# Graph layers of two batches interleaved ahead of the first attention, and the whole program written out by batch from a table

## The chip, the cores and the metric

One core of one Trainium2 chip runs the kernel. The metric is the device time of one execution in microseconds (us); three runs of the kernel before are at hand. The profile comes from one further look at one execution of it, with the hardware profiler on.

## The reference

For each of 4 batches, a two-layer graph attention runs over a context of 256 nodes, with the layer-normed `x` as its adjacency; its result is added to `x`. Then a layer norm and one transformer block follow (grouped-query attention with 16 heads on 4 key/value heads, then a top-2 mixture of 8 experts), again added to `x`.

```python
def gat_layer(x, adj, W, a_self, a_neigh, b):      # twice per batch; 8 heads of 32
    feat = jnp.einsum('nf,hfo->hno', x, W)
    e = (feat @ a_self)[:, :, None] + (feat @ a_neigh)[:, None, :]
    e = leaky_relu(e, 0.2) + -1e10 * (1.0 - adj)[None]
    out = jnp.einsum('hnm,hmo->hno', softmax(e), feat) + b[:, None, :]
    return elu(concat_heads(out))
x = x + gat(gat(ctx, layernorm(x)), layernorm(x))
h = rmsnorm(layernorm(x)); q, k, v = h @ qw.T, h @ kw.T, h @ vw.T
...
x = x + (hidden + moe_out)
```

## The kernel before

Two kinds of work are done for each batch. The **graph layers** (function `gat` of each engine) are laid out over 48 steps: layer 0 has its units at steps 5 to 12 and layer 1 at steps 28 to 35. A unit is two heads of one half of the nodes. TensorE (PE) makes the pairwise sums of a unit in the bank `zb` (L424), ScalarE (ACT) copies them to `zs` (L625), VectorE (DVE) applies the leaky relu to `lr` (L895) and adds the mask with a row minimum in `tt` (L904), GpSimd (POOL) subtracts that minimum (L735), PE turns the unit in `tb` (L432: four transposes), ACT takes the exponential into `gpT` (L630), and PE multiplies with the features in `ob` (L443: eight products of 33 columns). Ahead of the units of a layer stand the terms of the two attention vectors (L400), their three bf16 parts (L877 to L881, L408) and the features (L414); for layer 0 also the mask (L860 to L872). The layers end with the elu, the sum `x1`, and a preparation: a layer norm and an RMS norm whose inverse roots are iterated on POOL, and a transpose to `hT` (steps 44 to 47: L851, L937 to L950, L715 to L747, L455).

The **transformer block** (functions `fill`, `empty`, `part`) has steps of its own, from the QKV products (L509) at step 1 to the down products (L565) at step 47, in five PSUM banks.

The order on every engine is written by hand, as loops over the steps: first the graph layers of batch 0 alone (here called the **prologue**), then three turns of a hardware loop (**passes** 0, 1 and 2) whose step `s` holds step `s` of the graph layers of batch `b + 1` and step `s` of the block of batch `b`, then the block of batch 3 alone (the **last pass**). Each engine works strictly in its order and waits on semaphores. The loop is one body that all engines jump back to, with semaphore values worked out in registers:

```python
            for s in range(STEPS):
                ...
                gat(0, s)
            with pe.Fori(0, B - 1) as b:
                for s in range(STEPS):
                    gat(b + 1, s)
                    for w in work(s):
                        fill(b, w)
                    long_products(b, s)
            for s in range(STEPS):
                for w in work(s):
                    fill(B - 1, w)
                long_products(B - 1, s)
```

Of the kernel before, what the change touches and what calls it, by code (L numbers as in the profile page):

```python
# [7 lines left out]
BF16 = mybir.dt.bfloat16  # L8
ALU = mybir.AluOpType
# [26 lines left out]
C_CAUSAL = C_ID + P  # L36
C_COS = C_CAUSAL + P
C_SIN = C_COS + T * HD
C_PICK = C_SIN + T * HD
# [4 lines left out]
C_END = C_TRI + E * E  # L44
# [28 lines left out]
N_A, N_B, N_P = 39, 64, 36  # L73


STEPS = 48

# [71 lines left out]
BANKS = SLOW_BANKS + QUICK_BANKS  # L149
ORDER = [w for s in range(STEPS) for w in work(s)]  # L150
# [10 lines left out]
def block_program(nc, x, ctxT, w0, w1, gat_rows, norm_cols, qk_rows, wqkv, wo, wgate, wgu, wd, consts, spread, out):  # L161
    ctx = ExitStack()
    with ctx:
# [10 lines left out]
        cst = sb("cst", [P, C_END])  # L174
# [8 lines left out]
        qkw = sb("qkw", [P, 2 * HD])  # L183
# [8 lines left out]
        xin = sb("xin", [P, T, D])  # L192
        cin = sb("cin", [F_IN, N])
        stats = sb("stats", [P, T, 6])
        mv = sb("mv", [P, T, 2])
        rs_v = sb("rs_v", [P, 2 * T])
        rs_y = sb("rs_y", [P, 2 * T])
        rs_a = sb("rs_a", [P, 2 * T])
        maskv = sb("maskv", [P, T, N])
        feat = sb("feat", [P, T, H, FE])  # L200
        sn_res = sb("sn_res", [P, T, 2 * H])
        parts = sb("parts", [P, T, NP, 2 * H], BF16)
        partsT = sb("partsT", [KZ, N], BF16)
        pair_l = sb("pair_l", [KZ, N], BF16)
        pair_r = sb("pair_r", [KZ, H, N], BF16)
        zs = sb("zs", [P, 2, 2 * N])
        lr = sb("lr", [P, 2, 2 * N])
        tt = sb("tt", [P, 3, 2, N])
        gmn = sb("gmn", [P, 3, 2])
        gpT = sb("gpT", [P, 3, 2, T, P])  # L210
        gsum = sb("gsum", [P, H])
        go = rows[:, 2 * D:4 * D].rearrange("p (t d) -> p t d", t=T)
        gex = sb("gex", [P, T, D])
        wprod = gex[:, 0, :]
        x1 = sb("x1", [P, T, D])
        hid = sb("hid", [P, T, D])
        hn = gex
        hT = sb("hT", [P, KT, N])
        gT = hT
# [3 lines left out]
        v_sb = sb("v_sb", [P, T, HKV * HD])  # L223
        m1 = sb("m1", [P, 4, G * HD])
        m2 = sb("m2", [P, 4, G * HD])
        ssq = sb("ssq", [P, QU * G])
# [6 lines left out]
        qT = sb("qT", [P, HQ, N])  # L233
        kT = sb("kT", [P, HKV, N])
# [4 lines left out]
        prob = sb("prob", [P, 5, 2 * N])  # L239
        pT0 = sb("pT0", [P, G, P])  # L240
        pT1 = sb("pT1", [P, T, G, P])
# [14 lines left out]
        mixT = sb("mixT", [NP * E, N], BF16)  # L256
# [6 lines left out]
        zb = pb("zb", [P, 512])  # L263
        tb = pb("tb", [P, 512])
        ob = pb("ob", [P, 512])
        bank = [pb(f"bank{k}", [P, 512]) for k in range(BANKS)]


        in_cst, in_w0, in_gat, in_x, in_c = sem("in_cst"), sem("in_w0"), sem("in_gat"), sem("in_x"), sem("in_c")
        in_qkv, in_o, in_gu, in_d = sem("in_qkv"), sem("in_o"), sem("in_gu"), sem("in_d")  # L270
        out_free = sem("out_free")
        x_used, c_used = sem("x_used"), sem("c_used")

        setup_v, setup_done = sem("setup_v"), sem("setup_done")

        dve_a = sem("dve_a")
        z_full, z_free = sem("z_full"), sem("z_free")
        t_full, t_free = sem("t_full"), sem("t_free")
        parts_ready, pair_l_ready = sem("parts_ready"), sem("pair_l_ready")
        pair_r0_ready, pair_r1_ready = sem("pair_r0_ready"), sem("pair_r1_ready")  # L280
        lrelu_done, score_ready, shifted = sem("lrelu_done"), sem("score_ready"), sem("shifted")
        pv_done, o_free = sem("pv_done"), sem("o_free")
        gout_ready, gexp_ready, gres_ready, hn_ready = sem("gout_ready"), sem("gexp_ready"), sem("gres_ready"), sem("hn_ready")
        ln_seed, pool_a, ln_ready, hid_ready = sem("ln_seed"), sem("pool_a"), sem("ln_ready"), sem("hid_ready")
# [17 lines left out]
        def t_value(b, l, n):  # L302


            return b * 2 * (NU + 3) + l * (NU + 3) + n + 1

# [38 lines left out]
        def _(sp):  # L345
            sp.dma_start(w0x[:, 0:D], w0).then_inc(in_w0, 16)
            sp.dma_start(rows[:, 0:2 * D], gat_rows[:, 0:2 * D]).then_inc(in_w0, 16)
            sp.dma_start(cst[:, :], consts).then_inc(in_cst, 16)
            sp.dma_start(cin[:, :], ctxT[0]).then_inc(in_c, 16)
            sp.dma_start(xin[:, :, :], x[0].rearrange("(t p) d -> p t d", p=P)).then_inc(in_x, 16)  # L350
# [4 lines left out]
            sp.dma_start(qkw[:, :], qk_rows).then_inc(in_gat, 16)  # L355
# [7 lines left out]
            def load_inputs(b):  # L363
                sp.wait_ge(c_used, b)
                sp.dma_start(cin[:, :], ctxT[bass.ds(b, 1)].squeeze(0) if not isinstance(b, int) else ctxT[b]).then_inc(in_c, 16)
                sp.wait_ge(x_used, b)
                src = x[bass.ds(b, 1)].squeeze(0) if not isinstance(b, int) else x[b]
                sp.dma_start(xin[:, :, :], src.rearrange("(t p) d -> p t d", p=P)).then_inc(in_x, 16)

            def store(b):  # L370
                dst = out[bass.ds(b, 1)].squeeze(0) if not isinstance(b, int) else out[b]
                for t in range(T):
                    sp.wait_ge(y_ready, b * T + t + 1)
                    sp.dma_start(dst[t * P:(t + 1) * P, :], yo[:, t, :]).then_inc(out_free, 16)

            load_inputs(1)
            with sp.Fori(0, B - 2) as b:
                load_inputs(b + 2)
                store(b)
            store(B - 2)  # L380
            store(B - 1)
# [4 lines left out]
        def _(pe):  # L386
            def gat(b, a):

                for l in range(2):
                    operands = [(cin, w0x)] if l == 0 else [(gT[:, k, :], w1x[:, k, :]) for k in range(KT)]  # L390
                    if a == TERMS_AT[l]:
                        if l == 0:
                            pe.wait_ge(in_c, (b + 1) * 16)
                        else:
                            pe.wait_ge(t_free, t_value(b, 0, NU + 2) + 1)
                            pe.nop(nofuse=True)
                        pe.wait_ge(t_free, t_value(b, l, 0))
                        for t in range(T):
                            for i, (xt, w) in enumerate(operands):
                                mm = pe.matmul(tb[:, t * 2 * H:(t + 1) * 2 * H], xt[:, t * P:(t + 1) * P], w[:, D:D + 2 * H],  # L400
                                               start=(i == 0), stop=(i == len(operands) - 1))
                        mm.then_inc(t_full, 1)
                    if a == PARTS_AT[l]:
                        pe.wait_ge(parts_ready, b * 2 + l + 1)
                        pe.wait_ge(t_free, t_value(b, l, 1))
                        pe.nop(nofuse=True)
                        for t in range(T):
                            mm = pe.transpose(tb[0:KZ, t * P // 2:(t + 1) * P // 2].bitcast(BF16),  # L408
                                              parts[:, t, :, :].rearrange("p a c -> p (a c)"), identb[:, :])
                        mm.then_inc(t_full, 1)  # L410
                        pe.wait_ge(z_free, z_value(b, l, 0))
                        for t in range(T):
                            for i, (xt, w) in enumerate(operands):
                                mm = pe.matmul(zb[:, t * D:(t + 1) * D], xt[:, t * P:(t + 1) * P], w[:, 0:D],  # L414
                                               start=(i == 0), stop=(i == len(operands) - 1))
                        mm.then_inc(z_full, 1)
                    for k in units(l, a):
                        t, hp = divmod(k, H // 2)
                        if k == 0:
                            pe.wait_ge(pair_l_ready, b * 2 + l + 1)  # L420
                        if k < H // 2:
                            pe.wait_ge(pair_r0_ready if k < 2 else pair_r1_ready, b * 4 + l * 2 + k % 2 + 1)
                        pe.wait_ge(z_free, z_value(b, l, k + 1))
                        pe.matmul(zb[:, :], pair_l[:, t * P:(t + 1) * P],  # L424
                                  pair_r[:, 2 * hp:2 * hp + 2, :].rearrange("k h m -> k (h m)"), start=True, stop=True)\
                          .then_inc(z_full, 1)
                    for k in units(l, a - TRANS_LAG):
                        pe.wait_ge(shifted, unit(b, l, k) + 1)
                        pe.wait_ge(t_free, t_value(b, l, k + 2))
                        for h in range(2):  # L430
                            for m in range(T):
                                mm = pe.transpose(tb[:, (h * T + m) * P:(h * T + m + 1) * P],  # L432
                                                  tt[:, k % 3, h, m * P:(m + 1) * P], ident)
# [802 lines left out]
```

## Time and profile before

| | |
|---|---|
| runs | 679.01 us median of 3 (676.33, 679.01, 680.93) |
| profiled execution, span from first to last instruction | 676.1 us |
| mean granted TensorE clock | 0.944 |
| PE busy | 604.8 us (89%) |
| DVE busy | 441.0 us (65%) |
| POOL busy | 292.0 us (43%) |
| ACT busy | 266.7 us (39%) |

Of the profiled execution the span is the time that is known; it is 0.2 us under the fastest run and 2.9 us under the median. PE is the busiest engine, but the share is a mean over stages with different limits, so the stages are to be read one by one: the prologue up to the first QKV product at 100.21 us, the three passes, and the last pass from 559.00 us.

### The profile page before, as it was taken

Reading aid. Unit: us, or ns where it says so; the run is one execution under the profiler, and the core shown is the slowest. Engines: PE = TensorE matmul, PEld = TensorE weight load, DVE = VectorE, ACT = ScalarE, POOL = GpSimd, SP = SyncE. Lnnn points to the kernel's source line nnn. Section 1 sums busy time; section 2 is a strip of 40 time slices with the busy share of each in tenths; the row PEclk is TensorE's granted clock in tenths of the full one; section 3 lists DMA queues with packets and bytes.
Section 4 is the critical chain, followed back from the end, with each engine's and each line's share of the span. In section 5 each row is a group of like instructions: output and inputs, shape, how many; then the busy total and the mean of one; then the engine's idle time right before and its main releaser. Section 6 shows DMA issues by size and latency. Waiting matters only on the chain.

```text
span 676.1 us, 11574 instructions
## 1 busy us (share of the span) xinstructions
PE 604.8 (89%) x3140; PEld 445.9 (66%) x3140; DVE 441.0 (65%) x1277; ACT 266.7 (39%) x653; POOL 292.0 (43%) x588
## 2 busy tenths in 40 slices
PE   2786938979999998879999998879999998999998
PEld 1573933559678873558778973458777974676786
DVE  5727537975738756985738765986738766565363
ACT  2313305546533304636633304647633303674020
POOL 1514325885424023886425023886424126773000
PEclk9997558898999998979999998989999999999999
DMA  8900000000000000000000000000000000000000
GB/s 313 380 6 0 2 16 4 1 2 1 0 1 2 2 26 10 4 0 2 0 1 1 1 26 10 1 0 1 1 1 1 1 1 16 1 1 1 1 1 16
DMA packets 8305, 14.51 MB, mean 21 GB/s; under 512 B 860, under 2 KB 7068, under 8 KB 7988
## 3 DMA queue, kind: packets, MB, share of 16 engines
q1 hardware_dynamic: 8244, 13.76, 5.8%
q8 instruction: 31, 0.51, 0.3%
q14 instruction: 30, 0.25, 0.1%
HBM read 12.70 MB, written 1.05 MB: 20 GB/s over the span
## 4 chain that ended last, share of the span: by engine, by line
PE 56%; DVE 16%; issue 13%; POOL 9%; ACT 4%; POOLq 1%; DMA 1%; DVEq 0%; ACTq 0%; SPq 0%
PE bank L565 10%; PE bank L463 9%; PE ob L443 9%; PE bank L523 5%; PE tb L432 5%; PE bank L542 4%; DVE tt L904 3%; POOL m L775 2%; PE bank L538 2%; PE bank L534 2%; PE bank L509 2%; DVE lr L895 2%; PE zb L424 1%; ACT prob L666 1%; PE zb L414 1%
## 5 line engine op out<-in xcount | busy, mean ns | idle before, releaser
L735 POOL TENSOR_SCALAR tt<-tt,gmn 128x256 f32<-128x256 f32 x128 | 77.1, 613 | 64.1 <-DVE gmn L904 63.5
L509 PE MATMUL bank<-wqkv_sb,hT 128*128 128x512 f32 x192 | 97.9, 648 | 0.0
L666 ACT ACTIVATE prob<-bank,sneg,rms 128x128 f32<-128x128 f32 (+1 forms) x128 | 64.0, 507 | 68.5 <-DVE sneg L995 67.7
L775 POOL TENSOR_TENSOR m<-early,rope_s 128x256 f32<-128x256 f32 x80 | 70.8, 908 | 42.1 <-ACT early L647 41.8
L463 PE MATMUL bank<-m,wgu_sb 128*128 128x128 f32 (+1 forms) x480 | 86.6, 330 | 1.0 <-DVE m L1025 0.6
L791 POOL TENSOR_SCALAR prob<-prob,srcp 128x128 f32<-128x128 f32 (+1 forms) x128 | 53.7, 436 | 55.5 <-DVE srcp L1066 55.4
L463 PEld LDWEIGHTS bank<-m,wgu_sb 128*128 128x128 f32 x480 | 71.2, 191 | 9.2 <-issue 2.2
L443 PEld LDWEIGHTS ob<-feat,gpT 128*128 128x128 f32 x512 | 75.8, 227 | 0.8 <-issue 0.6
L443 PE MATMUL ob<-feat,gpT 128*128 128x33 f32 x512 | 75.2, 297 | 0.0
L895 DVE SCALAR_TENSOR_TENSOR lr<-zs 128x512 f32<-128x512 f32 x64 | 50.9, 797 | 25.3 <-ACT zs L625 22.6
L904 DVE CUSTOM_DVE_ANT_0 tt<-lr,maskv 128x256 f32<-128x256 f32 x128 | 62.3, 522 | 3.5 <-issue 2.9
L523 PE MATMUL bank<-kT,qT 128*128 128x128 f32 (+1 forms) x256 | 62.3, 360 | 0.9 <-ACT prob L666 0.9
L625 ACT ACTIVATE zs<-zb 128x512 f32<-128x512 f32 x64 | 38.3, 599 | 59.7 <-PE zb L424 56.5
L509 PEld LDWEIGHTS bank<-wqkv_sb,hT 128*128 128x128 f32 x192 | 36.3, 203 | 38.0 <-issue 35.0
L565 PE MATMUL bank<-wo_sb,qT 128*128 128x256 f32 x256 | 59.7, 383 | 0.3 <-ACT qT L672 0.3
L647 ACT ACTIVATE early<-bank 128x512 f32<-128x512 f32 x40 | 24.1, 603 | 89.8 <-PE bank L509 89.8
L565 PEld LDWEIGHTS bank<-wo_sb,qT 128*128 128x128 f32 x256 | 47.3, 190 | 10.0 <-issue 4.5
L432 PE MATMUL tb<-cst,tt 128*128 128x128 f32 x256 | 48.8, 322 | 4.6 <-ACT gpT L630 3.8
L523 PEld LDWEIGHTS bank<-kT,qT 128*128 128x128 f32 x256 | 41.4, 199 | 12.4 <-issue 6.3
L994 DVE TENSOR_REDUCE smx<-bank 128x2 f32<-128x512 f32 (+1 forms) x48 | 33.0, 686 | 24.8 <-PE bank L525 21.8
L630 ACT ACTIVATE gpT<-tb 128x512 f32<-128x512 f32 x64 | 38.4, 599 | 20.4 <-PE tb L432 19.9
L432 PEld LDWEIGHTS tb<-cst,tt 128*128 128x128 f32 x256 | 34.5, 169 | 17.1 <-issue 7.6
(151 smaller groups left out, 1026.5 us busy)
## 6 DMA issues: line engine op xcount, KB each, us to landing
wqkv_sb<-wqkv_dram SPq DMA_DIRECT2D x1, 3072.0 KB, 12.4
wgu_sb<-wgu_dram SPq DMA_DIRECT2D x2, 1408.0 KB, 11.2
wo_sb<-wo_dram SPq DMA_DIRECT2D x1, 2048.0 KB, 17.8
wd_sb<-wd_dram SPq DMA_DIRECT2D x1, 1408.0 KB, 15.6
xin<-x_dram SPq DMA_DIRECT2D x4, 256.0 KB, 2.7
out_dram<-rows SPq DMA_DIRECT2D x8, 128.0 KB, 1.9
rows<-gat_rows_dram SPq DMA_DIRECT2D x1, 512.0 KB
cst<-consts_dram SPq DMA_DIRECT2D x1, 425.0 KB, 3.6
```

The costliest lines, as they stand in the source:

```text
L432: mm = pe.transpose(tb[:, (h * T + m) * P:(h * T + m + 1) * P], tt[:, k % 3, h, m * P:(m + 1) * P], ident)
L443: mm = pe.matmul(ob[:, hh * FE:(hh + 1) * FE], gpT[:, k % 3, h, m, :], feat[:, m, hh, :], start=(m == 0), stop=(m == T - 1))
L463: mm = pe.matmul(ps[:, m * N + c0:m * N + c1], wgu_sb[:, m, k, n * P:(n + 1) * P], tokT[:, k, c0:c1], start=(k == 0), stop=(k == KT - 1))
L509: mm = pe.matmul(ps[:, :], hT[:, k, t * P:(t + 1) * P], wqkv_sb[:, k, c * G * HD:(c + 1) * G * HD], start=(k == 0), stop=(k == KT - 1))
L523: pe.matmul(ps[:, i * nk:(i + 1) * nk], qT[:, G * g + h, t * P:(t + 1) * P], kT[:, g, 0:nk], start=True, stop=False)
L565: mm = pe.matmul(bank_of(w)[:, 0:D], lhs[:, k, t * P:(t + 1) * P], rhs[:, k, :], start=(k == 0), stop=(k == end - 1))
L666: ins = act.activation(prob[:, n % 5, i * nk:(i + 1) * nk], ps[:, i * nk:(i + 1) * nk], ACT.Exp, bias=sneg[:, n, i:i + 1], scale=rq(g, t, ...
L735: ins = pool.tensor_scalar(tt[:, k % 3, h, :], tt[:, k % 3, h, :], -1.0, gmn[:, k % 3, h:h + 1], ALU.mult, ALU.add)
L775: ins = pool.tensor_tensor(dst[:, :, c, :], src[:, :, 1 - c, :], s_, ALU.mult)
L791: ins = pool.tensor_scalar(part_, part_, srcp[:, n, i:i + 1], 1.0, ALU.mult, ALU.mult)
L895: dve.scalar_tensor_tensor(lr[:, k % 2, :], zs[:, k % 2, :], 0.2, zs[:, k % 2, :], ALU.mult, ALU.min)\
L904: ins = dve.tensor_tensor_reduce(tt[:, k % 3, h, :], lr[:, k % 2, h * N:(h + 1) * N], maskv[:, t, :], 1.0, 3e38, ALU.add, ALU.min, gmn[:, ...
```

## The change

A table `PLAN` lists, step by step, whose work each engine issues, and every engine walks it without a loop. Ahead of the first block it holds the graph layers of batches 0 and 1, those of batch 1 two steps behind (`BEHIND`), and the preparation of batch 0. Pass 0 then carries the graph layers of batch 2, pass 1 those of batch 3, and passes 2 and 3 carry none; the preparation (`prep`) of the next batch stays at steps 44 to 47 of each pass.

For that, two sets of graph-layer buffers and semaphores exist. Set 0 (batches 0, 2 and 3) has buffers of its own; set 1 (batch 1 alone) is laid into tiles of the transformer block that are not in use yet (`qT`, `kT`, `v_sb`, `prob`, `pT0`, `pT1`) and into the PSUM banks 0 to 2. `x1` has three buffers, so that the sums of later batches can wait. `gT` and `hT` no longer share a tile. To make room, the rotary and causal tables are loaded into `x1` and `hid` at the start, and not kept in `cst`; this makes two more transfers in the setup, and the inputs of batch 1 are loaded there too.

```diff
+SET, SEQ, XS = (0, 1, 0, 0), (0, 0, 1, 2), 3
+BEHIND = 2
+PLAN = []
+for step in range(STEPS):
+    PLAN += [("gat", 0, step), ("gat", 1, step - BEHIND), ("prep", 0, step)]
...
+        PLAN += [("gat", batch + 2, step)] if batch + 2 < B else []
+        PLAN += [("prep", batch + 1, step)] if batch + 1 < B else []
+        PLAN += [("tail", batch, step)]
...
+        zb, tb, ob = [zb0, bank[0]], [tb0, bank[1]], [ob0, bank[2]]
...
+            sp.dma_start(angles, consts[:, C_COS:C_CAUSAL]).then_inc(in_gat, 16)
+            sp.dma_start(causal_in, consts[:, C_CAUSAL:C_END]).then_inc(in_gat, 16)
...
-            with pe.Fori(0, B - 1) as b:
-                for s in range(STEPS):
-                    gat(b + 1, s)
+            for what, b, s in PLAN:
+                if what == "gat":
...
+                    gat(b, s)
+                elif what == "prep":
+                    prep(b, s)
+                else:
...
                     for w in work(s):
                         fill(b, w)
                     long_products(b, s)
```

**PE, in the middle of layer 0.** Names are those of the tiles; tiles of set 1 read `bank`, `qT`, `v_sb`, `pT`, `prob`. Before, with L424 the sums, L432 the transposes and L443 the products of 33 columns:

```order
L424 MATMUL zb<-pair_r,pair_l 128x512
L432 MATMUL tb<-cst,tt 128x128 x4
L443 MATMUL ob<-feat,gpT 128x33 x4
L424 MATMUL zb<-pair_r,pair_l 128x512
L432 MATMUL tb<-cst,tt 128x128 x4
```

Now, with L464, L472 and L483 for the same three:

```order
L464 MATMUL zb<-pair_r,pair_l 128x512
L472 MATMUL tb<-cst,tt 128x128 x4
L483 MATMUL ob<-feat,gpT 128x33 x4
L464 MATMUL bank<-v_sb,pT 128x512
L472 MATMUL bank<-cst,qT 128x128 x4
L483 MATMUL bank<-pT,prob 128x33 x4
```

Each step now holds the three operations for batch 0 and then the same three for batch 1.

**PE, between the two layers.** Before, where L455 is the transpose of the layer's result, L400 and L408 the terms and their parts, L414 the features:

```order
L443 MATMUL ob<-feat,gpT 128x33 x8
L455 MATMUL tb<-cst,gex 128x128 x4
L400 MATMUL tb<-w1x,hT 128x16 x4
L408 MATMUL tb<-identb,parts 48x128 x2
L414 MATMUL zb<-w1x,hT 128x256 x4
L424 MATMUL zb<-pair_r,pair_l 128x512 x5
```

Now, where L491, L440, L448 and L454 are those four:

```order
L483 MATMUL bank<-pT,prob 128x33 x8
L491 MATMUL tb<-cst,gex 128x128 x4
L440 MATMUL tb<-w1x,gT 128x16 x4
L491 MATMUL bank<-cst,prob 128x128 x4
L448 MATMUL tb<-identb,parts 48x128 x2
L454 MATMUL zb<-w1x,gT 128x256 x4
L440 MATMUL bank<-w1x,kT 128x16 x4
L448 MATMUL bank<-identb,parts 48x128 x2
L454 MATMUL bank<-w1x,kT 128x256 x4
L464 MATMUL zb<-pair_r,pair_l 128x512 x3
L464 MATMUL bank<-v_sb,pT 128x512
```

The products of batch 1 stand ahead of batch 0's transpose, and the openings of the two layers 1 alternate.

**DVE, ahead of the first unit.** Before, from the last Newton step (L846) and the mask (L870, L872) on, with L895 the leaky relu and the ISA rows of L904 the masked minimum:

```order
L846 SCALAR_TENSOR_TENSOR rs_y<-rs_a,rs_y 128x2
L870 TENSOR_SCALAR maskv<-xin,mv,rs_y 128x256 x2
L872 TENSOR_SCALAR maskv<-maskv 128x512
L895 SCALAR_TENSOR_TENSOR lr<-zs 128x512 x2
L904 ISA tt,gmn<-lr,maskv 128x256
```

Now, from the same mask on:

```order
L915 TENSOR_SCALAR maskv<-maskv 128x512
L903 BN_STATS stats<-kT 128x6 x2
L894 BN_AGGR mv<-stats 128x2 x2
L906 TENSOR_SCALAR rs_v<-mv 128x2
L882 TENSOR_SCALAR rs_a<-rs_v 128x2
L883 TENSOR_SCALAR rs_y<-rs_a 128x2
L927 COPY pT<-bank 48x256
L929 TENSOR_SCALAR pT<-pT,cst 48x256
L938 SCALAR_TENSOR_TENSOR lr<-zs 128x512
L887 SCALAR_TENSOR_TENSOR rs_a<-rs_y 128x2
```

Between batch 0's mask and its first masked minimum, DVE now works on batch 1's moments, parts and Newton steps.

## Rows read from the trace of the kernel before

**Rows 1.** Stages: stretch and length; busy PE, PEld, DVE, ACT, POOL; clock; DMA

```profile
0.00:100.21 100.21, 62.84 (x248) 50.22 (x248) 53.85 (x175) 26.60 (x47) 31.84 (x58) 0.80 0.34 121
100.21:253.11 152.90, 145.73 (x786) 106.55 (x785) 108.30 (x312) 65.86 (x163) 72.78 (x146) 0.96 0.02 4
253.11:406.36 153.25, 144.29 (x787) 105.75 (x786) 108.68 (x312) 65.97 (x163) 72.30 (x146) 0.97 0.02 5
406.36:559.00 152.64, 143.67 (x782) 105.59 (x782) 108.32 (x311) 65.98 (x163) 72.27 (x146) 0.97 0.01 3
559.00:676.10 117.10, 108.31 (x542) 77.77 (x540) 61.85 (x167) 42.34 (x117) 42.78 (x92) 0.99 0.01 4
```

**Rows 2.** The prologue cut where PE becomes or ceases to be full, same columns

```profile
0.00:7.80 7.80, 0.00 (x0) 0.00 (x0) 2.01 (x7) 1.28 (x1) 0.19 (x4) 1.00 0.70 226
7.80:26.00 18.20, 8.85 (x24) 4.47 (x25) 15.51 (x53) 6.56 (x12) 7.29 (x9) 1.00 1.05 377
26.00:45.80 19.80, 19.80 (x91) 18.36 (x90) 7.55 (x26) 5.68 (x10) 6.16 (x12) 1.00 0.42 161
45.80:57.20 11.40, 7.07 (x23) 5.18 (x22) 6.53 (x22) 0.42 (x1) 2.44 (x4) 1.00 0.00 0
57.20:67.90 10.70, 5.27 (x16) 2.25 (x16) 8.47 (x25) 6.56 (x12) 4.70 (x5) 0.66 0.00 0
67.90:87.70 19.80, 19.77 (x91) 18.32 (x90) 8.46 (x28) 5.68 (x10) 6.12 (x12) 0.50 0.01 2
87.70:100.21 12.51, 2.08 (x8) 1.64 (x8) 5.32 (x17) 0.42 (x1) 4.95 (x14) 0.50 0.07 21
```

**Rows 3.** Timeline of PE, prologue, layer 1: start, us, operation, count, idle before

```profile
69.55 0.60 PE L424 MATMUL zb<-pair_r,pair_l 48*128 48x512 bf16 x1
70.09 1.11 PE L432 MATMUL tb<-cst,tt 128*128 128x128 f32 x4
70.99 1.75 PE L443 MATMUL ob<-feat,gpT 128*128 128x33 f32 x8
72.68 0.60 PE L424 MATMUL zb<-pair_r,pair_l 48*128 48x512 bf16 x1
```

**Rows 4.** Timeline of PE, prologue, layer 0

```profile
31.35 1.11 PE L432 MATMUL tb<-cst,tt 128*128 128x128 f32 x4
32.26 1.75 PE L443 MATMUL ob<-feat,gpT 128*128 128x33 f32 x8
```

**Rows 5.** Timeline of PE, pass 0, a unit of batch 1

```profile
145.00 0.39 PE L424 MATMUL zb<-pair_r,pair_l 48*128 48x512 bf16 x1
145.31 0.66 PE L432 MATMUL tb<-cst,tt 128*128 128x128 f32 x4
145.81 0.98 PE L443 MATMUL ob<-feat,gpT 128*128 128x33 f32 x8
146.62 0.31 PE L517 MATMUL bank<-cst,m 128*128 128x128 f32 x1
```

**Rows 6.** Timeline of PE, prologue, features of layer 1 and sums after them

```profile
53.44 3.78 PE L414 MATMUL zb<-w1x,hT 128*128 128x256 f32 x8
58.93 0.37 PE L424 MATMUL zb<-pair_r,pair_l 48*128 48x512 bf16 x1 [1.71 <-ACT pair_r L618]
61.76 0.58 PE L424 MATMUL zb<-pair_r,pair_l 48*128 48x512 bf16 x1 [0.78 <-ACT zs L625]
```

**Rows 7.** Batch 0's parts, moments and mask on DVE, columns of rows 1

```profile
8.87:11.98 3.11, 2.10 (x6) 1.32 (x6) 2.72 (x13) 0.00 (x0) 0.00 (x0) 1.00 1.00 358
15.97:18.94 2.97, 0.67 (x2) 0.10 (x1) 2.62 (x12) 0.60 (x1) 0.00 (x0) 1.00 0.98 349
```

**Rows 8.** Timelines of DVE and PE at the second jump back of the loop

```profile
409.53 0.19 DVE L877 CAST parts<-tb 128x32 bf16<-128x32 f32 x1 [3.32 <-issue]
...
411.10 0.27 PE L408 MATMUL tb<-identb,parts 128*48 128x128 bf16 x2 [2.76 <-DVE parts L881]
```

**Rows 9.** Timeline, last products of the last pass

```profile
666.24 7.17 PE L565 MATMUL bank<-wd_sb,early 128*128 128x256 f32 x32
```

More of the change, by code:

```diff
@@ L3 @@
 from contextlib import ExitStack
+import math
 import numpy as np
@@ L149 @@
 BANKS = SLOW_BANKS + QUICK_BANKS
+PLAN = []
+for step in range(STEPS):
+    PLAN += [("gat", 0, step), ("gat", 1, step - BEHIND), ("prep", 0, step)]
+for batch in range(B):
+    for step in range(STEPS):
+        PLAN += [("gat", batch + 2, step)] if batch + 2 < B else []
+        PLAN += [("prep", batch + 1, step)] if batch + 1 < B else []
+        PLAN += [("tail", batch, step)]
 ORDER = [w for s in range(STEPS) for w in work(s)]
@@ L204, in block_program @@
[L204 to L215, printed above, removed]
+        stats = [sb(f"stats{i}", [P, T, 6]) for i in range(2)]
@@ new lines, in block_program @@
+        mv = [sb(f"mv{i}", [P, T, 2]) for i in range(2)]
+        rs_v = [sb(f"rs_v{i}", [P, T]) for i in range(2)]
+        rs_y = [sb(f"rs_y{i}", [P, T]) for i in range(2)]
+        rs_a = [sb(f"rs_a{i}", [P, T]) for i in range(2)]
+        gmn = [sb(f"gmn{i}", [P, 3, 2]) for i in range(2)]
+        gsum = [sb(f"gsum{i}", [P, H]) for i in range(2)]
+        sn_res = [sb(f"sn_res{i}", [P, T, 2 * H]) for i in range(2)]
+        parts = [sb(f"parts{i}", [P, T, NP, 2 * H], BF16) for i in range(2)]
@@ new lines, in two @@
+        def two(name):
+            return [sem(f"{name}{i}") for i in range(2)]
+        in_x, in_c, x_used, c_used = two("in_x"), two("in_c"), two("x_used"), two("c_used")
+        z_full, z_free = two("z_full"), two("z_free")
+        t_full, t_free = two("t_full"), two("t_free")
+        parts_ready, pair_l_ready = two("parts_ready"), two("pair_l_ready")
+        pair_r0_ready, pair_r1_ready = two("pair_r0_ready"), two("pair_r1_ready")
+        lrelu_done, score_ready, shifted = two("lrelu_done"), two("score_ready"), two("shifted")
@@ L361, in _ @@
             sp.dma_start(wd_sb[:, :, :], wd.rearrange("(j p) n -> p j n", p=P)).then_inc(in_d, 16)
[L363 to L378, printed above, removed]
+            for b in range(2, B):
+                load_inputs(b)
+            for b in range(B):
                 store(b)
-            store(B - 2)
-            store(B - 1)
             sp.wait_ge(out_free, 16 * T * (B + 1))
@@ L387, in gat @@
             def gat(b, a):
+                i, q = SET[b], SEQ[b]
                 for l in range(2):
[L390 removed]
+                    operands = [(cin[i], w0x)] if l == 0 else [(gT[i][:, k, :], w1x[:, k, :]) for k in range(KT)]
                     if a == TERMS_AT[l]:
                         if l == 0:
[L393 removed]
+                            pe.wait_ge(in_c[i], (q + 1) * 16)
@@ L600, in _ @@
                     long_products(b, s)
-            for s in range(STEPS):
-                for w in work(s):
-                    fill(B - 1, w)
-                long_products(B - 1, s)
         @block.scalar
@@ L682, in empty @@
                     act.activation(th[:, n % 3, :], ps[:, 0:N], ACT.Tanh, scale=0.5).then_inc(tanh_ready, 1)
-            for s in range(STEPS):
-                gat(0, s)
-            act.wait_ge(setup_done, 3)
-            with act.Fori(0, B - 1) as b:
-                for s in range(STEPS):
-                    gat(b + 1, s)
+            for what, b, s in PLAN:
+                if what == "gat":
+                    gat(b, s)
+                elif what == "tail":
+                    if b == 0 and s == 0:
+                        act.wait_ge(setup_done, 3)
                     for w in use(s):
                         empty(b, w)
-            for s in range(STEPS):
-                for w in use(s):
-                    empty(B - 1, w)
         @block.gpsimd
@@ L794, in _ @@
             pool.wait_ge(setup_done, 1)
-            for s in range(STEPS):
-                gat(0, s)
-            pool.wait_ge(setup_done, 3)
-            with pool.Fori(0, B - 1) as b:
-                links[0] = 0
-                for s in range(STEPS):
-                    gat(b + 1, s)
+            for what, b, s in PLAN:
+                if what == "gat":
+                    gat(b, s)
+                elif what == "prep":
+                    prep(b, s)
+                else:
+                    if b == 0 and s == 0:
+                        pool.wait_ge(setup_done, 3)
                     for w in use(s):
@@ L804, in _ @@
                     normalise(b, s)
-            assert links[0] == N_P, links
-            links[0] = 0
-            for s in range(STEPS):
-                for w in use(s):
-                    part(B - 1, w)
-                normalise(B - 1, s)
-        A_LINKS, B_LINKS = [0], [0]
         @block.vector
@@ L1189, in _ @@
                     reciprocals(b, s)
-            assert count[1] == N_B, count
-            count[:] = [0, 0]
-            for s in range(STEPS):
-                for w in use(s):
-                    part(B - 1, w)
-                second_norm(B - 1, s)
-                reciprocals(B - 1, s)
+            assert count[1] == B * N_B, count
 def kernel(**inputs):
```

462 lines of the change are left out of this document (249 added, 213 removed).

## The prediction

> **What bounds the kernel now.** I read the stages first. The prologue, with the graph layers of one batch, takes 100.21 us; each pass, with a block and the layers of the next batch, takes 152.90, 153.25 and 152.64 us; the last pass, a block alone, takes 117.10 us [rows 1]. In the passes PE is busy for 143.67 to 145.73 us, at a granted clock of 0.96 to 0.97: they are PE's. The prologue holds PE work of only 62.84 us, so it looks like a stage with 37 us to give away. That is the case for the change: put a second batch into those holes, and pass 2 no longer has to carry its layers.
>
> So the next thing to read is what the holes are. Cut where PE becomes full, the prologue has PE idle for 7.80 us at the start, 9.35 us up to 26.00, 4.33 us between the layers, 5.43 us while layer 1 starts, and 10.43 us at the end; in the two long stretches of units, 26.00 to 45.80 and 67.90 to 87.70, PE is busy 19.80 and 19.77 us of 19.80 [rows 2]. Those two are half of PE's time in the prologue, and there nothing waits but for PE.
>
> Then its clock there. In layer 1 the granted clock is 0.50 [rows 2], which is the 1.2 GHz level: from one unit's sums to the next it is 72.68 - 69.55 = 3.13 us, with four transposes in 1.11 us and eight products of 33 columns in 1.75 us [rows 3]. In layer 0 the clock column says 1.00, but the same operations take 1.11 and 1.75 us there as well [rows 4], against 0.66 and 0.98 us for the same in pass 0 [rows 5], where the unit takes 146.62 - 145.00 = 1.62 us. So layer 0 ran at 1.2 GHz too, and the 1.00 there is only what the record holds before its first entry. What PE did in those stretches is graph units and nothing else, without a hole, for almost 20 us each, and the clock did not rise. It did rise right after the features of layer 1, eight products of 256 columns in 3.78 us: the next sums take 0.37 us, and those of 61.76, after more idle time, 0.58 us again [rows 6]. So what is in PE's queue counts, not only that it is full.
>
> A rule of the Trainium skill speaks the other way: "TensorE: Matmul & The Clock Gate", section "What's actually happening", says that the default state is throttled and that sustained activity releases it; read simply, a PE without holes runs at 2.4 GHz. These two stretches disagree. By the rule the time would be that of the first rival, below.
>
> **The change, part by part.** The sum is made against the span of 676.1 us.
>
> *Prologue.* PE gets the second batch's layers. Their work is that of the first without the last stretch, 62.84 - 2.08 = 60.8 us at 1.2 GHz [rows 2]. Against that stand the holes it may fill. The first 7.80 us stay (DMA and setup on DVE), and the last 10.43 us stay: DVE issues the preparation only after batch 1's last elu, then come POOL's iterations and two transposes, as now. The three in between sum to 9.35 + 4.33 + 5.43 = 19.1 us. I do not expect most of it. Up to 26.00 DVE is busy for 15.51 of 18.20 us [rows 2], and the new order puts batch 1's parts, moments and Newton steps ahead of batch 0's first masked minimum; batch 0's own took 3.11 + 2.97 us [rows 7], and about 4.9 us of such a row come earlier than the first unit. PE's first transposes come so much later, and what PE can do meanwhile for batch 1 (terms, features, sums) is about 5 us: nothing gained. Between the layers the openings alternate, which hides most waits; but the rotary tables are built on DVE right there, between batch 0's parts and batch 1's, so that I take 2.5 us of the 4.33. At the start of layer 1, batch 1 adds two sums to the ramp: 2 us of the 5.43. Filled: 4.5 us, bounds 0 and 19.1. And the features of the two batches, twice 3.78 us with little between, may bring the clock up for the second of them: 1.5 us, bounds 0 and 3. The prologue grows by 60.8 - 4.5 - 1.5 = **54.8 us** (38.7 to 60.8), to about 155 us.
>
> In the stretches of units DVE, ACT and POOL have room: twice the DVE time of 26.00 to 45.80 is 15.1 us [rows 2], against PE's 39.6 us for the same.
>
> *Passes.* Pass 0 carries the layers of batch 2 in place of batch 1's, pass 1 those of batch 3; both keep their work. Pass 2 loses them. What is left is the last pass up to its last products: these end at 666.24 + 7.17 = 673.41 [rows 9], 114.4 us after 559.00, and the preparation of batch 3, which stays at its steps, adds four transposes on PE, about 0.5 us as in rows 5 (145.31 to 145.81). Its DVE and POOL part runs beside the experts and the down products as it does in the passes now; without that cover it would cost what the last stretch of rows 2 lasts beyond 7.17 us of down products, some 5 us. So pass 2 falls from 152.64 to 114.9 us: **-37.7 us** (-39 to -33).
>
> *No loop.* At the second jump back DVE starts its parts 3.32 us late with nothing to wait for, and PE waits 2.76 us for them [rows 8]. The entry of pass 1 is straight code now, and PE's wait there should go. Pass 0 is entered without a jump already and is hardly shorter [rows 1], but it starts at the low clock. I take **-2.7 us** for pass 1 (-4 to 0); that of pass 2 has gone with its layers. The register instructions ahead of the waits go as well; PE idles for only 7.2 to 9.0 us in a pass [rows 1], so **-1 us** (-5 to 0).
>
> *At no cost:* the two more transfers of the setup and batch 1's inputs, since DVE works without a hole on other things until it needs them (up to 1 us if they land late); the longer program, since the last pass is straight code as well and shows no hole of that kind; three buffers of `x1`, which only take waits away.
>
> Sum: +54.8 - 37.7 - 2.7 - 1.0 = **+13.4 us**, a span of 689.5 us. The median of the runs is 2.9 us over the profiled span; so I forecast **692 us**. The exchange is easily told: 37.7 us are saved where PE does the layers at 2.4 GHz beside other work, and some 55 us are paid where it does them alone at 1.2 GHz.
>
> **The rivals.**
>
> 1. *The clock rises* (faster). If PE, fuller than before, is granted 2.4 GHz through the units of both layers, a unit falls to 1.62 us [rows 5] and DVE becomes the bound: its 53.85 us of the prologue, 108.30 - 61.85 = 46.5 us for a second batch [rows 1], and its idle time at start and end, 5.8 and 7.2 us [rows 2], with some 2 us between, make 115 us. That is +15 in place of +54.8: 652 us. It decides from the point at which the mix of rows 3 raises the clock. For it: the second batch closes the holes at the openings. Against it: the mix itself is the same, and it ran twice for almost 20 us without a hole and did not rise. This is the case that the Trainium skill's rule would give.
> 2. *The clock rises after the features and holds in layer 1.* With two batches' features the level may be kept into the units. Layer 1's start and units then go from some 53 us of PE to twice the DVE time of 57.20 to 87.70, 33.9 us [rows 2]: 19 us less, 673 us; 682 if it holds half way. Against it: the sums that open the units leave PE mostly idle, and after just such sums the clock fell [rows 6].
> 3. *The sets do not overlap* (slower still). PE's queue is one row for both sets; if each wait of one holds the other at every step, batch 1 costs the whole 87.70 - 7.80 = 79.9 us: 25 us more, 717 us. Against it: the lags of several steps are kept, and each set has its own buffers.
> 4. *Pass 2 doesn't gain* since another bound shows there. The last pass is the proof against: the same block in 117.10 us.
>
> **How the numbers follow.** The forecast has 0.73, rival 2 has 0.11, rival 1 has 0.08, rival 3 with lesser stalls of its kind 0.07, rival 4 0.01. The forecast's own range, from the bounds that are likely together (0 to 9 us filled, the passes 4 us better or worse), is 683 to 701; with most of rival 2 and a little of rival 3 the range for 8 in 10 is 676 to 703. A measurement of this kernel tells about 1% from no change (the runs lie within 0.7%). Slower by over 1% means above 685.8: nearly all of the forecast and rival 3, 0.71. Within 1% is 672.2 to 685.8: the forecast's low end and most of rival 2, 0.17. Faster by over 1%: rival 1 and the rest, 0.12.
>
> **What would show it.** In the changed profile the first QKV products should start near 155 us, not near 115; the time from one unit of a set to its next in mid-layer should be about 6.2 us at a granted clock of 0.50; four transposes should take 1.1 us; PE should be full from about 31 us to the end of layer 0. Pass 1 should be some 3 us shorter than now, passes 2 and 3 should take 115 and 117 us. A unit pair in 3.5 us at 1.00 would mean rival 1, and I would have been wrong on what raises the clock.

## The result and the profile after

The changed kernel takes 687.78 us (median of 4 runs, 687.37 to 688.63) against 677.67 us of the kernel before: a recorded ratio of 1.0136, with a 95% interval of 1.0102 to 1.017 (the two medians alone would give 1.0149). It is slower by 1.4%; the forecast was 692 us. The profiled span went from 676.1 to 686.8 us, by 10.7 us.

The stages of the changed kernel, cut at the first QKV products of each batch; the columns are those of rows 1 (stretch, length, busy PE, PEld, DVE, ACT, POOL with their instructions, clock, DMA):

```profile
0.00:160.06 160.06, 120.02 (x488) 98.98 (x489) 95.00 (x313) 51.06 (x93) 66.51 (x98) 0.81 0.22 78
160.06:310.24 150.18, 144.00 (x787) 105.84 (x786) 107.22 (x312) 66.40 (x163) 73.04 (x146) 0.97 0.01 4
310.24:458.35 148.11, 142.73 (x782) 105.22 (x782) 106.68 (x311) 66.41 (x163) 73.21 (x146) 0.98 0.01 3
458.35:571.42 113.07, 106.91 (x547) 77.73 (x546) 64.31 (x176) 42.33 (x117) 47.86 (x106) 1.00 0.01 3
571.42:686.80 115.38, 106.62 (x542) 77.15 (x540) 61.92 (x167) 42.34 (x117) 42.90 (x92) 1.00 0.01 4
```

Against [rows 1]: the prologue is 59.85 us longer; pass 0 is 2.72, pass 1 5.14, pass 2 39.57 and the last pass 1.72 us shorter. The five sum to +10.70 us, the whole change of the span.

The same prologue cut where PE becomes or ceases to be full, as in [rows 2]:

```profile
0.00:8.10 8.10, 0.00 (x0) 0.00 (x0) 2.14 (x9) 1.28 (x1) 0.19 (x4) 1.00 0.61 167
8.10:35.53 27.43, 13.22 (x38) 7.24 (x38) 21.59 (x79) 10.64 (x20) 8.96 (x13) 1.00 1.04 379
35.53:77.80 42.27, 42.27 (x193) 38.59 (x192) 22.92 (x75) 13.89 (x25) 21.54 (x28) 1.00 0.03 10
77.80:94.09 16.29, 13.52 (x45) 10.43 (x46) 10.17 (x33) 2.97 (x6) 4.62 (x8) 1.00 0.00 1
94.09:104.98 10.89, 6.50 (x19) 2.43 (x18) 7.76 (x23) 7.97 (x15) 5.62 (x6) 0.68 0.00 0
104.98:147.40 42.42, 42.42 (x192) 38.65 (x191) 25.09 (x79) 13.89 (x25) 20.61 (x27) 0.50 0.03 7
147.40:160.06 12.66, 2.09 (x9) 1.64 (x9) 5.32 (x17) 0.42 (x1) 4.98 (x14) 0.50 0.00 0
```

Two stretches of more than 42 us now have PE busy to the last digit. Idle time of PE in the prologue is 160.06 - 120.02 = 40.0 us, where it was 37.4: the second batch has not made the holes smaller. The one at the start grew from 9.35 to 14.21 us, the one between the layers shrank from 4.33 to 2.77 us, the opening of layer 1 from 5.43 to 4.39 us; the first 8 us and the end are 0.4 us longer together.

The timeline of PE in the middle of layer 1 of the changed kernel (start, us, operation):

```profile
114.95 0.60 PE L464 MATMUL bank<-v_sb,pT 48*128 48x512 bf16 x1
115.48 1.12 PE L472 MATMUL bank<-cst,qT 128*128 128x128 f32 x4
116.39 1.76 PE L483 MATMUL bank<-pT,prob 128*128 128x33 f32 x8
117.96 1.09 PE L472 MATMUL tb<-cst,tt 128*128 128x128 f32 x4
118.85 1.75 PE L483 MATMUL ob<-feat,gpT 128*128 128x33 f32 x8
120.53 0.60 PE L464 MATMUL bank<-v_sb,pT 48*128 48x512 bf16 x1
```

Four transposes in 1.09 to 1.12 us and eight products in 1.75 us are the durations of [rows 3], at a granted clock of 0.50: the 1.2 GHz level. From one sum of batch 1 to its next it is 5.58 us for two units: one with a sum, 3.13 us as in [rows 3], and one without, which leaves 2.45 us. Batch 0's eight sums had all been made by 112.4 us, in the opening of the layer and the first units, so the pair is shorter than the 6.2 us of the forecast.

### The profile page after: what moved, and what is told of

Same layout as the page of the kernel before. It is cut to its first block, busy times and chain, and to the rows that moved or that the text cites. A ratio compares the mean times of both kernels' runs of the same rounds, so it can differ in the third digit from the quotient of the medians.

```text
span 686.8 us, 10097 instructions
## 1 busy us (share of the span) xinstructions
PE 620.3 (90%) x3140; PEld 464.9 (68%) x3140; DVE 435.1 (63%) x1279; ACT 268.5 (39%) x653; POOL 303.5 (44%) x588
## 4 chain that ended last, share of the span: by engine, by line
PE 65%; DVE 17%; POOL 6%; issue 5%; ACT 4%; DMA 1%; SPq 1%; DVEq 0%; POOLq 0%; ACTq 0%
PE bank L611 14%; PE bank L509 9%; PE ob L483 7%; PE bank L569 5%; PE bank L588 4%; PE tb L472 4%; PE bank L483 4%; PE bank L555 3%; PE bank L472 2%; DVE ssq L1012 2%; PE bank L584 2%; PE bank L580 2%; ACT prob L715 2%; DVE tt L947 2%; DVE m L1009 2%
## 5 line engine op out<-in xcount | busy, mean ns | idle before, releaser
L555 PE MATMUL bank<-wqkv_sb,hT 128*128 128x512 f32 x192 | 91.7, 616 | 0.8 <-ACT v_sb L691 0.8
L783 POOL TENSOR_SCALAR tt<-tt,gmn 128x256 f32<-128x256 f32 x96 | 67.7, 715 | 37.2 <-DVE gmn L947 36.8
L483 PEld LDWEIGHTS ob<-feat,gpT 128*128 128x128 f32 x384 | 60.6, 239 | 0.1
L483 PE MATMUL ob<-feat,gpT 128*128 128x33 f32 x384 | 59.7, 307 | 0.0
L938 DVE SCALAR_TENSOR_TENSOR lr<-zs 128x512 f32<-128x512 f32 x48 | 37.3, 778 | 18.5 <-ACT zs L674 17.8
L947 DVE CUSTOM_DVE_ANT_0 tt<-lr,maskv 128x256 f32<-128x256 f32 x96 | 46.2, 516 | 2.2 <-issue 2.2
L472 PE MATMUL tb<-cst,tt 128*128 128x128 f32 x192 | 38.4, 334 | 4.2 <-POOL tt L783 2.7
L1009 DVE TENSOR_TENSOR m<-early,rope_c 128x512 f32<-128x512 f32 x40 | 29.4, 735 | 19.4 <-ACT early L696 19.4
L674 ACT ACTIVATE zs<-zb 128x512 f32<-128x512 f32 x48 | 28.7, 598 | 32.6 <-PE zb L464 31.2
L761 POOL TENSOR_TENSOR ln_a<-ln_y 128x4 f32<-128x4 f32 x12 | 2.4, 200 | 87.1 <-DVEq L985 86.5
```

The costliest lines, as they stand in the source:

```text
L472: mm = pe.transpose(tb[i][:, (h * T + m) * P:(h * T + m + 1) * P], tt[i][:, k % 3, h, m * P:(m + 1) * P], ident)
L483: mm = pe.matmul(ob[i][:, hh * FE:(hh + 1) * FE], gpT[i][:, k % 3, h, m, :], feat[i][:, m, hh, :], start=(m == 0), stop=(m == T - 1))
L555: mm = pe.matmul(ps[:, :], hT[:, k, t * P:(t + 1) * P], wqkv_sb[:, k, c * G * HD:(c + 1) * G * HD], start=(k == 0), stop=(k == KT - 1))
L783: ins = pool.tensor_scalar(tt[i][:, k % 3, h, :], tt[i][:, k % 3, h, :], -1.0, gmn[i][:, k % 3, h:h + 1], ALU.mult, ALU.add)
L947: ins = dve.tensor_tensor_reduce(tt[i][:, k % 3, h, :], lr[i][:, k % 2, h * N:(h + 1) * N], maskv[i][:, t, :], 1.0, 3e38, ALU.add, ALU.min ...
L1009: ins = dve.tensor_tensor(m1[:, u % 4, :].rearrange("p (h d) -> p h d", h=G), raw[:, u % 3, :].rearrange("p (h d) -> p h d", h=G), c_, ALU ...
```

## The experiments

**Writing out alone (e4_unroll).** One batch in the prologue and the next batch's layers in passes 0 to 2, as in the kernel before, but walked from the table. The other edits of the changed kernel (three buffers of `x1`, `gT` and `hT` apart, the preparation as a part of its own) stay in; the edit also moves the loads of batches 1 to 3 and drops the waits for set 1, not shown here:

```diff
-SET, SEQ, XS = (0, 1, 0, 0), (0, 0, 1, 2), 3
+SET, SEQ, XS = (0, 0, 0, 0), (0, 1, 2, 3), 3
...
-    PLAN += [("gat", 0, step), ("gat", 1, step - BEHIND), ("prep", 0, step)]
+    PLAN += [("gat", 0, step), ("prep", 0, step)]
...
-        PLAN += [("gat", batch + 2, step)] if batch + 2 < B else []
+        PLAN += [("gat", batch + 1, step)] if batch + 1 < B else []
```

> Only the writing out by batch: the graph layers of batch 0 alone in the prologue, those of batches 1 to 3 in passes 0 to 2 as before, no loop, one set of buffers. Theory A: 2.7 us less at each of two jumps and 1 us or more less for the register instructions of each pass: 668 to 672 us, so that the interleaving by itself costs some 17 us. Rival, that writing out is worth nothing: 677 us, and the interleaving by itself costs 10 us.

Measured: 671.88 us, ratio 0.9888 (0.9812 to 0.9963). Its stages, same columns:

```profile
0.00:100.77 100.77, 62.74 (x249) 50.24 (x249) 53.81 (x177) 26.59 (x47) 31.84 (x58) 0.80 0.34 120
100.77:252.86 152.09, 145.38 (x787) 106.51 (x786) 106.93 (x312) 66.24 (x163) 72.88 (x146) 0.96 0.01 4
252.86:403.05 150.19, 143.33 (x787) 105.79 (x786) 106.92 (x312) 66.33 (x163) 72.97 (x146) 0.98 0.02 5
403.05:552.58 149.53, 142.68 (x782) 105.44 (x782) 106.52 (x311) 66.33 (x163) 72.96 (x146) 0.98 0.01 3
552.58:669.60 117.02, 108.32 (x542) 77.82 (x540) 61.84 (x167) 42.30 (x117) 42.76 (x92) 0.99 0.01 4
```

Against [rows 1] the passes entered by a jump before are 3.06 and 3.11 us shorter, pass 0 is 0.81, the last pass 0.08, and the prologue is 0.56 us longer. That is theory A: 671.88 us lies in its range, and moving the layers costs 15.9 us against the 17 expected. So the change is two things of opposite sign: writing out is worth 1.1% (0.4 to 1.9%), and moving the layers costs, from the two ratios, 1.0136 / 0.9888 = 1.025.

**Without the interleaving (e3_serial).** Batch 1's layers follow batch 0's:

```diff
-    PLAN += [("gat", 0, step), ("gat", 1, step - BEHIND), ("prep", 0, step)]
+    PLAN += [("gat", 0, step)]
+for step in range(STEPS):
+    PLAN += [("gat", 1, step), ("prep", 0, step)]
```

> The changed kernel with the graph layers of batch 1 behind those of batch 0 instead of interleaved. Theory A, that PE alone bounds the interleaved prologue and the interleaving fills only the openings of the layers: about 12 to 20 us longer, 700 to 708 us, with the units at 3.13 us each as in the kernel before. Rival, that the two sets hold each other in PE's queue and nothing is overlapped: the same time, 688 us or less.

Measured: 713.75 us, ratio 1.0506 (1.0423 to 1.0588). The first QKV products start at 181.30 us, 21.2 us later than with the interleaving: the sets do overlap, a little more than theory A said (700 to 708 us), and rival 3 of the prediction falls. Its second half, and two sums of neighbouring units in it:

```profile
100.20:181.30 81.10, 58.53 (x236) 47.81 (x236) 37.63 (x121) 22.17 (x40) 28.74 (x50) 1.00 0.00 1
```

```profile
150.58 0.60 PE L466 MATMUL bank<-v_sb,pT 48*128 48x512 bf16 x1
...
153.72 0.60 PE L466 MATMUL bank<-v_sb,pT 48*128 48x512 bf16 x1
```

A unit takes 3.14 us, as in [rows 3], and yet the clock column says 1.00 throughout: this prologue has no entry of the clock at all, so the column can't be trusted there and the durations decide.

**More columns in the same queue (e1_dense1, e2_dense4).** If it is the mix of PE's queue that keeps the clock at 1.2 GHz, then more dense work must raise it. Products of 512 bf16 columns are put behind each unit's transposes, into a bank that nobody reads in the prologue (`n` is 1 or 4):

```diff
                         mm.then_inc(t_full[i], 1)
+                        for _ in range(n if b < 2 else 0):
+                            pe.matmul(bank[4][:, :], identb[:, :], identb[:, :].unsqueeze(1).broadcast_to([P, 4, P]),
+                                      start=True, stop=True)
```

> The changed kernel with one extra product of 512 bf16 columns per unit in the prologue, into a PSUM bank that nobody reads there (32 in all). Theory A, that the mix in PE's queue keeps the clock at 1.2 GHz: the extra columns can only help; if one is enough the unit pair falls from 6.2 to about 3.7 us, the prologue from 160 to about 120 us and the time to about 650 us. If one is too few the products cost 32 times 0.43 us, 14 us: 702 us at a clock still of 0.50. Rival, that the clock is low in the prologue for another reason (early in the program, or holes in PE): 702 us whatever is added.

> The same with four extra products per unit (128 in all). Theory A: the clock rises to 1.00 in the units; a unit pair is then twice 1.62 us plus eight times 0.22 us, 5.0 us, against 6.2 now; prologue about 135 us, time about 663 us. Rival: the clock stays at 0.50, the products cost 128 times 0.43 us, 55 us: 743 us.

Measured: with one, 686.08 us, ratio 1.0093 (1.0059 to 1.0127), prologue 150.69 us; with four, 678.00 us, ratio 0.9997 (0.995 to 1.0044), prologue 148.08 us. Both do more work than the changed kernel with its 1.0136. The run with four is faster all the same; with one the two intervals overlap, though its prologue is 9.4 us shorter, since passes 0 and 1, whose code is the same, took 5.2 us longer in it. Neither came to the time that theory A gave (about 650 or 702 us with one, 663 us with four). Two stretches of the run with one product, the first in layer 0, the second in layer 1:

```profile
60.00:80.00 20.00, 20.00 (x91) 18.91 (x91) 5.71 (x19) 4.79 (x9) 1.87 (x4) 1.00 0.01 2
115.00:135.00 20.00, 19.03 (x152) 17.27 (x152) 18.05 (x58) 9.65 (x18) 17.80 (x23) 1.00 0.01 1
```

The clock column reads 1.00 in both, so the durations have to tell. Four transposes in either stretch:

```profile
63.02 1.09 PE L472 MATMUL tb<-cst,tt 128*128 128x128 f32 x4
119.49 0.66 PE L472 MATMUL tb<-cst,tt 128*128 128x128 f32 x4 [0.34 <-POOL tt L786]
```

In layer 0 they take 1.09 us, the 1.2 GHz level, and PE issues 91 products in 20 us; in layer 1, where the clock had come up at about 110 us, they take 0.66 us, and PE issues 152. One product per unit didn't raise the clock in layer 0, but kept it in layer 1; what had brought it up there isn't shown. With four it is up in the units of both layers:

```profile
45.00:70.00 25.00, 25.00 (x184) 20.16 (x184) 13.60 (x45) 8.85 (x17) 11.72 (x18) 1.00 0.01 2
105.00:130.00 25.00, 25.00 (x179) 19.39 (x177) 15.58 (x52) 9.94 (x18) 14.36 (x21) 1.00 0.01 2
```

Four transposes in the first of them:

```profile
57.62 0.63 PE L472 MATMUL tb<-cst,tt 128*128 128x128 f32 x4
```

Here PE is full, four transposes take 0.63 us in layer 0, and DVE is busy for 13.60 of 25 us: the extra products themselves are the bound now. Between the layers and at the end the granted clock is back at 0.50, and the prologue is 148 us and not the 135 of theory A. The rival of both runs, that nothing raises the clock there, falls.

**Four to raise, one to hold (e7_dense41; e8_unroll_dense).** The same edit with four products in the first three units of each layer and one in the others, in the changed kernel, and in the written-out kernel for its one batch. That makes 68 and 34 products in the traces; the texts put ahead of these runs count 56 and 28:

```diff
-                        for _ in range(n if b < 2 else 0):
+                        for _ in range((4 if k < 3 else 1) if b < 2 else 0):
```

> The changed kernel, two steps behind, with the same extra products, four in each of the first three units and one in each later one. Against the run with four everywhere (678 us) the later units lose three products of 0.22 us each: 80 fewer, some 15 us where PE is the bound; prologue about 133 us, time about 662 us. If one does not hold the clock: 678 us or more.

> Written out by batch, graph layers of batch 0 alone in the prologue as in the kernel before, with the same extra products for that batch (28 in all). Theory A: the clock rises in its units too; they are then bound by DVE and by the waits within one batch, not PE: prologue from 101 to about 86 us, time about 657 us. Rival, that a single batch has too many holes for the clock to hold: 101 us or more, 672 us.

Measured: 664.45 us, ratio 0.9781 (0.975 to 0.9811), prologue 132.83 us; and 660.87 us, ratio 0.9719 (0.9683 to 0.9755), prologue 92.85 us. The first in three stretches:

```profile
40.00:62.50 22.50, 22.50 (x179) 19.78 (x177) 18.26 (x58) 11.09 (x20) 17.93 (x23) 1.00 0.01 2
62.50:92.00 29.50, 22.22 (x83) 13.47 (x82) 20.29 (x62) 11.59 (x22) 12.62 (x16) 0.60 0.00 0
92.00:119.50 27.50, 27.50 (x212) 23.52 (x211) 22.47 (x72) 13.18 (x24) 19.53 (x25) 1.00 0.01 1
```

The first came out close to the 133 and 662 us expected. In the units the clock now holds (four transposes in 0.63 to 0.66 us); PE is still full there, and DVE is at 18.26 of 22.50 us. Between the layers it falls to 0.60 on the mean, and 29.50 us go by there. The written-out kernel is the fastest of these runs, though its prologue missed the 86 us expected: from 45 to 60 us, between its layers, the granted clock is 0.61. Against it, interleaving costs 40.0 us more of prologue and gives back 37.1 us in the passes, for a span of 662.2 against 659.3 us. So even where the clock is up in the units, the move of the layers doesn't pay: each of the four interleaved runs (664.02 to 664.84 us) is slower than each of the written-out kernel's (658.76 to 661.78), by 0.5% at the medians, though the intervals of the two ratios overlap.

**Six steps behind (e5_behind6, e6_behind6_dense).** Batch 1 further behind, and the preparation ahead of the layers, without and with the products four and one:

```diff
-BEHIND = 2
+BEHIND = 6
-    PLAN += [("gat", 0, step), ("gat", 1, step - BEHIND), ("prep", 0, step)]
+    PLAN += [("prep", 0, step), ("gat", 0, step), ("gat", 1, step - BEHIND)]
```

> The changed kernel with batch 1 six steps behind instead of two, and the preparation of batch 0 ahead of the graph layers in each step. No product is added. Theory A, a prologue that is PE's at 1.2 GHz with holes only at the start, between the layers, at the opening of layer 1 and at the end: batch 1's units now fill batch 0's openings (about 6 us) and its last units run beside the preparation (about 9 us of the last 12.7), so the prologue falls from 160 to about 145 us and the time to about 673 us. Rival, that the holes are set by DVE's order and move with it: less than 4 us, 684 us or more.

> The same six steps, and extra products of 512 bf16 columns in the prologue: four in each of the first three units of a layer and batch, one in each unit after that (56 in all). If four raise the clock and one holds it, as the runs with four and with one showed in part, the units are DVE's: prologue 115 to 125 us, time 645 to 655 us. If one does not hold it: the clock falls in mid-layer and the time is near 675 us.

Measured: 680.03 us, ratio 1.002 (0.9987 to 1.0053), prologue 147.62 us; and 666.06 us, ratio 0.9809 (0.9777 to 0.9841), prologue 135.72 us. The end of e5's prologue:

```profile
135.00:147.62 12.62, 11.36 (x53) 10.49 (x52) 7.30 (x23) 2.51 (x5) 5.65 (x15) 0.50 0.01 1
```

PE works 11.36 us of a stretch in which it worked 2.09 us in the changed kernel: batch 1's last units now run beside the preparation. That gives back 12.4 us of the prologue, near theory A (145 us expected); the time fell by 7.8 us only and missed the 673 us expected, in part since the last two passes take 677.4 - 446.2 = 231.2 us here, against 228.5. With the products the expectation failed (115 to 125 us of prologue, 645 to 655 us). The clock fell twice in the middle of units; here the stretch ahead of the first fall, and the two stretches after a fall:

```profile
35.00:40.00 5.00, 5.00 (x37) 3.95 (x36) 4.72 (x15) 2.76 (x5) 2.27 (x3) 1.00 0.32 113
42.00:52.00 10.00, 8.75 (x33) 6.54 (x34) 6.75 (x22) 2.81 (x5) 5.94 (x11) 0.50 0.01 2
103.00:113.00 10.00, 10.00 (x43) 7.69 (x42) 6.77 (x20) 3.75 (x7) 6.16 (x11) 0.55 0.00 1
```

Both times PE had been doing batch 0's units, with one product each, and of batch 1 the sums alone; the clock came back 10 to 13 us later, when batch 1's units with four had begun. Ahead of the first fall PE was busy for 5.00 of 5.00 us, so no hole ahead of it explains it. One product per unit held the clock in the runs above and not here; why isn't shown.

**Products in the gaps too (e9_after_hold, e10_unroll_hold).** To the edit of e7 and e8, in each kernel (`dense(n)` issues `n` of those products; the comments are added here):

```diff
+                        dense(4 if b < 2 and l == 1 else 0)     # after L440, the terms of layer 1
...
+                        dense(2 if b < 2 and k < 4 else 0)      # after L464, the first four sums
...
+                    dense(30 if b == 0 else 0)                  # ahead of L501, the first preparation
```

In e10 `b < 1` stands for `b < 2`.

> The changed kernel with extra products wherever the run with four and one lost the clock: four after the terms of layer 1, two after each of the first four sums of a layer, four and one after the transposes as before, and thirty ahead of the transposes of the first preparation. If the clock then holds at 1.00 from the first units to the first QKV products, the stretch between the layers goes at 2.4 GHz: prologue from 133 to about 122 us, time about 653 us, and the interleaving pays against the kernel written out alone with the same products. If the sums and the preparation are bound by DVE and POOL and not by PE: the products change nothing, 662 to 665 us.

> Written out by batch, one batch in the prologue, with the same extra products for that batch. The stretch between the layers and the opening of the block at the higher clock: prologue from 93 to about 88 us, time about 656 us. If DVE and POOL bound them: 660 us, no change.

Measured: 669.82 us, ratio 0.9862 (0.9815 to 0.9909), prologue 137.15 us; and 661.50 us, ratio 0.9739 (0.9686 to 0.9792), prologue 92.16 us. Both expectations of a gain fell. The gaps of e9, between the layers and ahead of the block:

```profile
65.00:90.00 25.00, 18.14 (x87) 11.47 (x86) 13.79 (x43) 8.44 (x18) 5.38 (x9) 0.86 0.00 1
124.00:137.15 13.15, 8.93 (x46) 4.72 (x45) 6.06 (x19) 0.42 (x1) 4.97 (x14) 0.91 0.07 20
```

The clock is higher there than in e7 and the gaps are no shorter: from the end of layer 0's products to the first products of layer 1 it is 28.47 us against 28.30, from the end of layer 1's products to the block 12.47 against 12.74. So the clock isn't what bounds them; PE waits in them for DVE and ACT, for DVE's parts alone 3.53 us. In e9 the prologue is even 4.3 us longer than in e7; 3.15 us of that arise ahead of layer 0's first products of 33 columns (38.38 against 35.23 us), where two extra products behind each sum took 1.04 us at the low clock.

## Why the prediction was right

**What bounds the prologue** was read rightly: PE at 1.2 GHz, with a mix that doesn't raise the clock however full it is. The trace after shows it in two stretches of 42 us, and the runs with one and four products show that it is the mix: the same units, with more columns among them, ran at 1.00. Rival 1, and with it the reading that a PE without holes is granted 2.4 GHz, is refuted for this mix. (A slip beside it: the two full stretches before are 39.57 of PE's 62.84 us, 63% and not half.) Rival 2 is refuted too: the clock came up after the second batch's features and fell in the sums that follow, as it had done in [rows 6]. That it rises there at all is not the rule: in e3 the sums after the features take 0.58 us in both batches. The timeline of PE there in the changed kernel:

```profile
90.38 3.78 PE L454 MATMUL bank<-w1x,kT 128*128 128x256 f32 x8
94.09 0.60 PE L464 MATMUL zb<-pair_r,pair_l 48*128 48x512 bf16 x1
95.47 0.37 PE L464 MATMUL zb<-pair_r,pair_l 48*128 48x512 bf16 x1 [0.78 <-ACT zs L674]
...
99.13 0.58 PE L464 MATMUL zb<-pair_r,pair_l 48*128 48x512 bf16 x1 [0.35 <-ACT zs L674]
```

**The prologue's term** was 54.8 us and came out at 59.85, just inside its bounds. PE was full from 35.53 us and not from about 31. Measured, the term is 57.18 us more of PE's busy time and 2.67 us more of its idle time. Three parts were mis-sized. The work, put at 60.8 us, came 3.6 us lower; in the full stretches a product costs 0.22 us before and after, so the difference lies in the openings, which I did not take apart. "Filled: 4.5 us" was in truth nothing: 2.6 us were filled at the layers' openings, and 4.9 us more were lost ahead of the first unit, where I had put the later start against PE's work for batch 1 and called it even. And the 1.5 us for a clock that rises in time for the second batch's features were not there: they took 3.78 us like the first.

**Pass 2** was to fall by 37.7 us and fell by 39.57, half a us beyond its bounds; the preparation is hidden there, as forecast. The passes without layers are shorter than I had read them, since the clock went another way at one place. In both kernels PE waits 2.67 us for the keys; in the kernel before, in the last pass, the clock falls after it:

```profile
572.13 0.79 PE L515 MATMUL bank<-cst,m 128*128 128x128 f32 x4 [2.67 <-DVE m L984]
572.71 3.49 PE L509 MATMUL bank<-wqkv_sb,hT 128*128 128x512 f32 x4
```

and in the changed kernel's pass 2 it doesn't:

```profile
471.49 0.66 PE L561 MATMUL bank<-cst,m 128*128 128x128 f32 x4 [2.67 <-DVE m L1030]
471.98 1.88 PE L555 MATMUL bank<-wqkv_sb,hT 128*128 128x512 f32 x4
```

3.49 against 1.88 us for the same four products is 1.6 us. The last pass, put at no change, is 1.72 us shorter by the same: its four products take 1.88 us too. The prediction could not know this from the one trace, and why it goes one way or the other isn't shown: at this place the last pass has 1.88 us in e1, e2 and e7, and 3.44, 3.19 and 3.54 us in e4, e8 and e10.

**No loop** was sized at -3.7 us in all, for the entry of pass 1 and the registers. By itself it gave 0.81 us in pass 0 and 3.06 us in pass 1, 3.9 us. The entry of pass 1 shows why: in the timeline of PE the parts follow at once, where at this entry they waited 2.55 us before (the 2.76 us of [rows 8] are at the entry of pass 2). First the kernel before, then the changed one:

```profile
257.64 0.27 PE L408 MATMUL tb<-identb,parts 128*48 128x128 bf16 x2 [2.55 <-DVE parts L881]
...
310.24 1.98 PE L555 MATMUL bank<-wqkv_sb,hT 128*128 128x512 f32 x4
312.15 0.29 PE L448 MATMUL tb<-identb,parts 128*48 128x128 bf16 x2
```

Passes 0 and 1 of the changed kernel are still some 2 us shorter each than those of the kernel that is only written out (150.18 and 148.11 against 152.09 and 150.19). In pass 1 PE idles for 5.4 us instead of 6.9; 1.55 us of it is one wait, of the transposes for ACT's `gpT`, 1.20 instead of 2.75 us. The plan alone doesn't give it: e1, with the same code in these passes, took 152.09 and 151.36 us. What causes it stays open.

**The sum** was +13.4 us of span and came out at +10.7: the prologue took 5 us more than its term, and the passes gave back some 8 us more than theirs. Of these 8 us, 1.9 are pass 2, 1.7 the last pass and 4.2 passes 0 and 1. That the time came within 4 us of the forecast is in part luck, then: two errors of opposite sign, one of them with a cause that stays open. The exchange was as told, 2.4 GHz beside other work given up for 1.2 GHz alone. Rival 1 was priced at 652 us, with a prologue of 115 us. The nearest run to it, e7 with the clock up in the units, has 132.8 us and 664 us: the gaps between the layers and at the end stay, and its 68 products are work for PE too. What the clock alone would give wasn't measured.

## What to carry to other kernels

A stage that looks half empty may be full where it counts: cut it at the points where the busiest engine becomes full, and price moved work at what the engine does there, with the clock of that place, not at what it does beside other work. A queue of narrow products can keep TensorE at its low level while it is busy without a hole; here 34 wide products that nobody needs took 11 us off the written-out kernel, 671.88 to 660.87 us. And a change of several parts should be measured in parts: here one gave 1.1% and the other took 2.5%.

## What the runs showed of the hardware that I had not expected

Adding work to the busiest engine shortened the time: with 128 more products PE's busy time in the prologue fell from 120.0 to 109.6 us, since the rest then ran at the higher level:

```profile
0.00:148.08 148.08, 109.60 (x616) 77.48 (x616) 95.54 (x313) 51.01 (x93) 66.65 (x98) 0.88 0.24 84
```

A mix that doesn't raise the clock may hold it: with one product per unit PE stayed at the low level in layer 0 and at the high level in layer 1, after it had come up there. It need not: in e6 units with one product lost the level twice. And the clock column can read 1.00 over 181 us in which every unit has the durations of the low level (e3_serial): ahead of the first entry of the record, the durations are the only evidence.
